# Attention slots in twos: unscaled exponentials are turned, and the reciprocals of the row sums go round by DRAM to the outputs' rows

## The reference

```python
xn = layernorm(x)
# attention
q = xn @ wq.T; lat = xn @ w_kv_down.T; k = lat @ w_k_up.T; v = lat @ w_v_up.T   # 16 heads of 64
q, k = rope(q), rope(k)
probs = softmax(q @ k.T / sqrt(64) + causal_mask)
s = concat_heads(probs @ v) @ wo.T
# experts
logits = xn @ gate_w + gate_b
e = max(top2_indices(logits))
y = gelu(xn @ w1[e] + b1[e]) @ w2[e] + b2[e]
out = x + s * silu(2 * y)
```

## Time and profile before

| | |
|---|---|
| median of 3 runs | 310.14 us (309.95 to 311.69) |
| the profiled execution's own time | 310.5 us |
| its span | 308.7 us |
| PE, busy share of the span | 95% |
| ACT, DVE, POOL | 79%, 72%, 70% |
| mean granted clock of PE | 0.998 |

### The profile page before, as it was taken

One profiled execution on the slowest core, in us unless ns is written; L12 is line 12 of the kernel. 1 busy time (PEld: TensorE's weight loads), 2 busy tenths in 40 slices (PEclk: granted clock), 3 DMA queues, 4 the chain that ended last, 5 costly groups with the idle time before them and its releaser, 6 DMA issues.

```text
span 308.7 us, 8487 instructions
## 1 busy us (share of the span) xinstructions
PE 294.3 (95%) x2362; PEld 235.4 (76%) x2362; DVE 221.0 (72%) x883; ACT 242.9 (79%) x851; POOL 215.9 (70%) x321
## 2 busy tenths in 40 slices
PE   8897999999999999999999989999989999899994
PEld 3566878888888888777777789999867777786763
DVE  3889998987787998988887523323278789898651
ACT  3387889898887889999897665555799999889982
POOL 3378878786786879999999933332138999889730
PEclk9999999999999999999999999999999999999999
DMA  6764595979333333333345470000063334344200
GB/s 204 232 140 112 107 308 124 225 168 302 74 69 71 68 71 89 92 87 87 99 104 134 129 197 0 2 2 0 3 187 71 93 102 115 103 108 133 71 19 17
DMA packets 39596, 33.35 MB, mean 108 GB/s; under 512 B 4801, under 2 KB 36674, under 8 KB 39554
## 3 DMA queue, kind: packets, MB, share of 16 engines
q1 hardware_dynamic: 38098, 30.51, 38.3%
q0 software_dynamic: 1024, 2.10, 2.5%
q10 hardware_dynamic: 432, 0.23, 0.3%
HBM read 11.07 MB, written 4.98 MB: 52 GB/s over the span
## 4 chain that ended last, share of the span: by engine, by line
PE 64%; POOL 12%; issue 11%; DVE 8%; ACT 2%; DMA 1%; POOLq 1%; SPq 0%; DVEq 0%; ACTq 0%
PE bank L1092 9%; PE bank L1080 8%; PE bank L1106 7%; PE bank L1120 6%; PE bank L1285 6%; PE bank L1300 6%; POOL probs L474 5%; POOL staged L463 4%; PE bank L1054 3%; DVE rot_out L585 3%; PE bank L1108 3%; PE bank L1082 3%; DVE masked L594 2%; PE bank L1188 2%; PE bank L1070 2%
## 5 line engine op out<-in xcount | busy, mean ns | idle before, releaser
L885 ACT ACTIVATE pexp<-masked,negmax 128x128 f32<-128x128 f32 (+1 forms) x256 | 114.1, 452 | 1.5 <-DVE negmax L594 1.4
L474 POOL TENSOR_SCALAR probs<-pexp,rden 128x256 f32<-128x256 f32 (+1 forms) x184 | 80.3, 451 | 26.0 <-DVE rden L601 23.3
L594 DVE CUSTOM_DVE_ANT_0 masked<-bank,mask 128x128 f32<-128x128 f32 (+1 forms) x256 | 75.9, 351 | 27.1 <-PE bank L1082 26.9
L463 POOL TENSOR_TENSOR staged<-rot_out 128x512 f32<-128x512 f32 x63 | 80.2, 1275 | 17.8 <-DVE rot_out L585 17.3
L585 DVE TENSOR_TENSOR rot_out<-bank,rot 128x1024 f32<-128x1024 f32 x64 | 77.6, 1214 | 4.0 <-PE bank L1056 2.7
L907 ACT COPY probsT<-bank 128x384 f32<-128x384 f32 x128 | 54.9, 480 | 22.9 <-PE bank L1092 21.9
L1092 PE MATMUL bank<-ident,probs 128*128 128x128 f32 x384 | 54.7, 275 | 1.8 <-ACT probsT L907 0.9
L885 ACT ACTIVATION_READ_ACCUMULATOR pexp<-masked,negmax 128x1 f32 x256 | 49.9, 195 | 0.0
L1080 PE MATMUL bank<-qk_sb 64*128 64x256 f32 x256 | 45.0, 427 | 2.9 <-DVE negmax L594 2.1
L1092 PEld LDWEIGHTS bank<-ident,probs 128*128 128x128 f32 x384 | 43.1, 140 | 5.2 <-POOL probs L474 1.9
L1120 PE MATMUL bank<-vo_sb,ctxT 128*128 128x128 f32 x256 | 39.4, 278 | 0.7 <-ACT ctxT L914 0.7
(11 more groups left out here) (113 smaller groups left out, 458.1 us busy)
## 6 DMA issues: line engine op xcount, KB each, us to landing
qk_sb<-staged SPq DMA_DIRECT2D x128, 128.0 KB, 2.5
w_sb<-in_w SPq DMA_DIRECT2D x2, 1024.0 KB, 5.6
w_sb<-in_w SPq DMA_DIRECT2D x4, 512.0 KB, 4.9
sorted_x<-z SPq DMA_DIRECT2D x1, 1408.0 KB, 7.9
sorted_g<-z SPq DMA_DIRECT2D x1, 1152.0 KB, 5.5
out<-res SPq DMA_DIRECT2D x8, 128.0 KB, 1.8
x_sb<-in_x SPq DMA_DIRECT2D x3, 256.0 KB, 3.8
rot<-in_c_rot SPq DMA_DIRECT2D x1, 512.0 KB, 5.0
```

The costliest lines, as they stand in the source:

```text
L463: pool.tensor_tensor(staged[:, n % 2, :, m % 2, :], rot_out[:, m % 2, :, 0:S], rot_out[:, m % 2, :, S:2 * S], op=ALU.add).then_inc(staged_ ...
L474: pool.tensor_scalar(probs[:, g % 2, i, c], pexp[:, g % 2, i, c], rden[:, g % 2, i, k:k + 1], 1.0, ALU.mult, ALU.mult).then_inc(probs_read ...
L594: t = dve.tensor_tensor_reduce(masked[:, g % 2, i, c], s_bank[i][:, c], mask[:, c], -1.0, -NEG * 1e8, ALU.add, ALU.min, negmax[:, g % 2, i ...
L885: e = act.activation(pexp[:, g % 2, i, c], masked[:, g % 2, i, c], ACT.Exp, bias=negmax[:, g % 2, i, k:k + 1], scale=-1.0, accum_out=rowsu ...
```

## The change

Slots from 24 on go in **couples** (`g` even, `g` and `g + 1`), one call of `couple(g)` on each engine in place of two of `slot`.

- PE: `scores_of_two(g + 2)` runs the four large matmuls of both slots and then the four corners, which now go to `t_bank`. Behind them stand the outputs of slots `g - 4` and `g - 3`, then a projection, `turn(g)`, the other projection, `turn(g + 1)`, and `values(g - 2)`.
- In slots 24 to 61 the exponentials are turned as they are (`pexp`), with no `scale`. DVE forms the contexts' copy and multiplies it by `shares`, the reciprocals laid along the rows (`ctx_out`, now one operation of 128x512 on DVE and none on ACT). Slots 62 and 63 are still scaled.
- `shares` comes by DRAM. SP writes the 128x8 reciprocals of a couple so that each number is an element of its own (`rows_out`), waits until they have landed, and reads them back spread over 64 partitions in two DMAs (`rows_back`).
- DVE takes the maxima in two steps, `corner_max` of both slots first and `rest_max` of each later. `turn(g)` waits for both corners to be read.
- `TWICE` is (23, 25), so two projections come earlier. Slots 38, 39, 62 and 63 are no longer alone.
- At the end of the couple of slot 38 `values(38)` uses a bank of the scores, and the second part of `load` has a semaphore of its own, `xs_rest`, and stands behind the `place` of the couple.

```diff
-TWICE = (36, 38)
+TWICE = (23, 25)
...
-ALONE = tuple(range(FIRST_DOUBLE)) + (G_LEAD - 2, G_LEAD - 1, B * NP - 2, B * NP - 1)
+ALONE = tuple(range(FIRST_DOUBLE))
+LAST = B * NP - 2
...
+def scaled(g):
+    return g < FIRST_DOUBLE or g >= LAST
...
+            def rows_out(u):
+                sp.wait_ge(rden_ready, 2 * u + 2)
+                sp.dma_start(share_rows[u].rearrange("n i k p -> p (n i k)"),
+                             rden[:, u % 2].rearrange("p n i k -> p (n i k)"),
+                             allow_slow_non_contiguous=True).then_inc(row_out, 16)
+            def rows_back(u):
+                sp.wait_ge(row_out, 16 * (u - UNIT + 1))
+                if u < UNIT + 2:
+                    sp.wait_ge(probsT_done, 2 * FIRST_DOUBLE)
+                else:
+                    sp.wait_ge(ctx_ready, values_through(2 * u - 4))
+                for i in range(2):
+                    sp.dma_start(shares[HD * i:HD * i + HD, u % 2],
+                                 share_rows[u, :, i].rearrange("n k p -> n (k p)").unsqueeze(0)
+                                 .broadcast_to([HD, 2, S])).then_inc(row_in[u % 2], 16)
...
+            def couple(g):
+                if g == G_LEAD - 2:
+                    sp.wait_ge(scattered, 16 * NT)
+                    load(0, 4, xs_in)
+                if g < LAST:
+                    rows_out(g // 2)
+                    rows_back(g // 2)
+                for m in (*items(g), *items(g + 1)):
+                    if m % 2:
+                        place(m // 2)
+                if g == G_LEAD - 2:
+                    load(4, NR, xs_rest)
+                for n in (g, g + 1):
+                    if n in FINALS:
+                        store(FINAL_ORDER.index(FINALS[n]))
...
+            def corner_max(g):
+                dve.wait_ge(scores_done, g + 1)
+                dve.wait_ge(exp_done, 2 * g - 6)
+                for i in range(2):
+                    t = dve.tensor_tensor_reduce(corner(g, i), t_bank[i][:, g % 2 * P:(g % 2 + 1) * P], mask[:, 0:P],
+                                                 -1.0, -NEG * 1e8, ALU.add, ALU.min, negmax[:, g % 4, i, 0:1])
+                t.then_inc(corner_read, 1)
+            def rest_max(g):
+                dve.wait_ge(exp_done, 2 * g - 2)
+                for i in range(2):
+                    dve.tensor_tensor_reduce(masked[:, g % 2, i, P:SW], s_bank[i][:, g % 2 * S:(g % 2 + 1) * S], mask[:, P:SW],
+                                             -1.0, -NEG * 1e8, ALU.add, ALU.min,
+                                             negmax[:, g % 4, i, 1:2]).then_inc(masked_ready, 1)
...
+            def ctx_out(g):
+                u = g // 2
+                dve.wait_ge(pv_done, values_through(g))
+                dve.wait_ge(y_step, g + 2 - NP)
+                o, heads = v_bank(g)[:, 0:2 * S], ctxT[:, g % NP:g % NP + 2, :].rearrange("p n s -> p (n s)")
+                if scaled(g):
+                    dve.tensor_copy(heads, o).then_inc(ctx_ready, 1)
+                else:
+                    dve.wait_ge(row_in[u % 2], 32 * ((u - UNIT) // 2 + 1))
+                    dve.tensor_tensor(heads, o, shares[:, u % 2].rearrange("p n s -> p (n s)"),
+                                      op=ALU.mult).then_inc(ctx_ready, 1)
+            def couple(g):
+                if g - 4 >= FIRST_DOUBLE and g not in (G_LEAD, G_LEAD + 2):
+                    ctx_out(g - 4)
+                if g < LAST:
+                    corner_max(g + 2)
+                    corner_max(g + 3)
+                denominators(g + 1)
+                if g == LAST:
+                    scale(g + 1)
+                if g < LAST:
+                    rest_max(g + 2)
+                for m in items(g):
+                    rotate(m)
+                if (g + 1) // NP < LEAD and (g + 1) % NP == 3:
+                    take_y((g + 1) // NP - 1)
+                if FINALS.get(g + 1, -1) >= LEAD:
+                    finalise(FINALS[g + 1])
+                if g < LAST:
+                    rest_max(g + 3)
+                    denominators(g + 2)
+                if g + 2 == LAST:
+                    scale(g + 2)
+                for n in range(g, g + 2):
+                    if FINALS.get(n, LEAD) < LEAD:
+                        finalise(FINALS[n])
+                if g in (G_LEAD - 2, LAST):
+                    ctx_out(g - 2)
+                for m in items(g + 1):
+                    rotate(m)
             def finish(b):
+                ctx_out(NP * b + NP - 2)
...
             def exponentials(g, i):
                 act.wait_ge(masked_ready, 2 * g + i + 1)
+                if g >= FIRST_DOUBLE + 2:
+                    act.wait_ge(probsT_done, 2 * g + i - 3)
+                    act.wait_ge(rden_ready, g - 1)
                 for k, c in enumerate(rows):
-                    wait(act, probs_ready[i][k], g - 1)
-                    e = act.activation(pexp[:, g % 2, i, c], masked[:, g % 2, i, c], ACT.Exp,
-                                       bias=negmax[:, g % 2, i, k:k + 1], scale=-1.0,
+                    if g < FIRST_DOUBLE + 2:
+                        wait(act, probs_ready[i][k], g - 1)
+                    e = act.activation(pexp[:, g % 2, i, c], masked[:, g % 2, i, c] if k else corner(g, i), ACT.Exp,
+                                       bias=negmax[:, g % 4, i, k:k + 1], scale=-1.0,
                                        accum_out=rowsum[:, g % 2, i, k:k + 1])
                 e.then_inc(exp_done, 1)
-
...
-                act.copy(ctxT[:, g % NP:g % NP + n, :].rearrange("p n s -> p (n s)"),
-                         o_bank[:, 0:n * S]).then_inc(ctx_ready, 1)
+                wait(act, y_step, g + 1 - NP)
...
+            def couple(g):
+                if g == FIRST_DOUBLE:
+                    exponentials(g + 1, 0)
                     ctx_out(g - 2)
-                if g == G_LEAD:
-                    exponentials(g + 1, 0)
-                ctx_out(g - 1)
-                if g == G_LEAD:
                     exponentials(g + 1, 1)
-                    scale(g + 1)
+                turned_probs(g)
+                if g < LAST:
+                    exponentials(g + 2, 0)
+                    if g != G_LEAD - 2:
+                        exponentials(g + 2, 1)
+                turned_probs(g + 1)
+                if g == G_LEAD - 2:
+                    exponentials(g + 2, 1)
+                if g < LAST:
+                    for i in range(2):
+                        exponentials(g + 3, i)
+                if g == FIRST_DOUBLE:
+                    ctx_out(g - 1)
...
+            def scores_of_two(g):
+                pe.wait_ge(masked_ready, 2 * g)
+                for n in range(2):
+                    p = (g + n) % NP
+                    pe.wait_ge(qk_in[p], 32 * (g // NP) + 32)
+                    for i, r in enumerate(half_rows):
+                        pe.matmul(s_bank[i][:, n * S:(n + 1) * S], qk_sb[r, 0, p, P:S], qk_sb[r, 1, p, :], start=True, stop=True)
+                pe.wait_ge(probsT_ready, 2 * (g - 2))
+                for n in range(2):
+                    p = (g + n) % NP
+                    for i, r in enumerate(half_rows):
+                        m = pe.matmul(t_bank[i][:, n * P:(n + 1) * P], qk_sb[r, 0, p, 0:P], qk_sb[r, 1, p, 0:P],
+                                      start=True, stop=True)
+                m.then_inc(scores_done, 2)
...
+            def couple(g):
+                ahead = (*items(g), *items(g + 1))
+                if g < LAST:
+                    scores_of_two(g + 2)
+                if g == FIRST_DOUBLE:
+                    output(g - 2)
+                elif g == FIRST_DOUBLE + 2:
+                    output(g - 3)
+                elif g not in (G_LEAD, G_LEAD + 2):
+                    output(g - 4)
+                    output(g - 3)
+                for m in ahead[:1]:
+                    project(m)
+                turn(g)
+                for m in ahead[1:2]:
+                    project(m)
+                if g == LAST:
+                    values(g - 2)
+                turn(g + 1)
+                for m in ahead[2:]:
+                    project(m)
+                if g == FIRST_DOUBLE:
+                    values(g - 1)
+                elif g not in (G_LEAD, LAST):
+                    values(g - 2)
+                if g == G_LEAD - 2:
+                    values(g)
...
             def finish(b):
                 g = NP * b + NP
+                output(g - 4)
+                output(g - 3)
                 if g == G_LEAD:
-                    output(g - 3)
-                output(g - 2)
-                values(g - 1)
-                if g == G_LEAD:
-                    pe.wait_ge(masked_ready, 2 * G_LEAD + 4)
                     pe.wait_ge(xs_in, 16)
                     turn_tile(0, 0)
+                else:
+                    values(g - 2)
+                output(g - 2)
                 output(g - 1)
```

173 lines of the change are left out of this document (85 added, 88 removed).

## The result

The changed kernel takes **464.22 us** (median of 4 runs, 463.76 to 464.79) beside 310.5 for the kernel before (four runs now): ratio 1.494 (95% interval 1.489 to 1.499). I had said 314, range 303 to 330. Medians and ranges are of all executions of a kernel, a ratio is of those within 1.5% of its fastest, and a time with no range beside it is of a single execution.

What follows compares the result with a forecast made beforehand. PE's own stream bounded the kernel before; the new couples were to follow a 6.88 us loop. Terms +3.5 - 0.5 + 2.0 - 1.3 = +3.7 on 310.5 gave 314.2, from the median 313.8, said as 314, range 303 to 330.

Steps and rivals of the forecast that it cites:

- D: Time from issue to landing of the store of a couple's reciprocals, which SP waits out: taken as 3.3 us.
- small elements dear: Rival: storing 4-byte pieces costs more than reading them; D 4.8, SP's round 8.7, total 333 to 337 us; chance 0.17.
- SP's round as D + 3.9: SP's queue per couple: the store's landing, then reads and place; 7.2 us against a couple of 6.9.
- the way to the experts: Slots 24 to 39: SP's rounds put the eighth `rows_out` at 171.4 and delay the experts by 3.5 us.
- The stream of 6.53: PE's own work per couple if nothing waits: fewer array changes take 0.40 us out of 6.93.
- The loop of 6.88: From `turn(g)` to `turn(g + 2)` over ACT, DVE and PE: 6.88 us a couple, outputs waiting 0.35.
- step 1: Loop's start on ACT: copy 0.58 after the transpositions, second at most 0.43 later, exponentials some 0.38 behind: 1.33 us.
- The experts' start at 180.1: Experts start behind `shares` at 178.25, `ctx_out(38)` at 178.95 and PE's last outputs (1.05), against 176.65 before: +3.5 us.
- D + 3.15: Time from the start of `rows_out` until the reciprocals read back have landed as `shares`.
- Behind the experts: Deferred outputs of three slots -0.5 us, six couples from 44 to 54 +2.0, couples 56, 58 and 60 -1.3.
- the end: The kernel's last stretch, one store behind one `finalise`, claimed to stay as before.
- waits on `shares` in every couple, and couples of 8 us or more: Sign in the profile after that would show the small elements rival, chance 0.17.

Runs made afterwards that it cites:

- two edits: On the 32 B version, rotate ahead of the last reciprocals: 320.67 us. The whole change with 16 B pieces and a strided multiplication: 327.41 us.
- the version with the fast store: The changed kernel with a couple's reciprocals stored as 128 pieces of 32 B instead of 1024 of 4 B, output wrongly scaled: 319.91 us.
- mended: Whole change with 16 B pieces (327.41 us), plus rotate, couple 38's store, ACT's copies of slots 40 and 41, and `ctx_out(58)` moved earlier: 321.21 us.
- finals: `mended` with DVE's finalise moved ahead of the couple's second rotate: 319.68 us.

## Why the prediction was wrong

1. **D, the landing of the reciprocals' store, is the step that failed.** I put it at 3.3 and closed the range at 3.8, by the load of 1024 small elements; it took 9.3 to 12.9, median 10.5. The bound was from a *read* of DRAM. The piece count was the same, but a load does not write 16 pieces into 64 B of DRAM; at one piece in 64 B the store did take 3.4. I named the rival (small elements dear), gave it 0.17 and held it at D of 4.8, less than half of what came; and the range ended at 330, below that rival's own 333 to 337.
2. **SP's round as D + 3.9** held in the changed kernel: 10.95 + 3.9 is 14.85, and 14.90 is in the rows. Put into my own working of the way to the experts, the eighth `rows_out` comes at 118.4 + 7 x 14.4 + 2.6 = 221.8 with the median (222.68 in the trace) and the experts start at 237.6 (0.4, 10.5, 3.15, 0.7 and 1.05 behind it); they start at 239.49, 62.8 later than before. From slot 40 to the end are 175.8 us against 85.8, 90 more. It did not hold beside quicker 4 B stores: with D at 3.4, near my own figure, the rounds were 8.1, the experts started at 188.33 and the kernel took 335.65, outside the range. So the right D alone would hardly have brought 314. The 22 us between were not taken apart further; that run also reads a table in place of the reciprocals.
3. **The stream of 6.53** was right in kind, 0.10 short (6.63). **The loop of 6.88** was right: 6.90 with a fast store, and it answered to two edits as a loop does. The wait there is 0.19 in the rows against my 0.35. (The parts of its step 1 are 0.58, at most 0.43, and 0.38, so up to 1.39; I wrote 1.33.)
4. **The experts' start at 180.1** is 180.22 in the version with the fast store, and that is luck. Its store of couple 38 starts at 170.27 and not 171.8; from there to `ctx_out(38)` are 7.34 us and not D + 3.15 = 6.45; and PE's outputs behind it, at half clock after a wait of 5.07, take 1.87 and not 1.05. With the store at 3.4 the start was 188.33.
5. **Behind the experts** I had -0.5, +2.0 and -1.3. With the fast store, slots 40 to 44 take 14.60 us against 13.08 before: the deferred outputs give nothing. PE's corners wait for ACT's copy of slot 41, which stands behind the `Silu`, a table load and the exponentials of 42 (PE's timeline of that version):

```profile
235.35 0.71 PE L1226 MATMUL bank<-qk_sb 64*128 64x128 f32 x8 [1.76 <-ACT probsT L1041]
```

   Most of the 1.5 us is PE's clock behind that wait, 0.74 in the mean from 235.35 to 241.87. In the run with pieces 64 B apart the same wait is 1.75 and the clock behind it 1.00, and the slots take 13.29. `mended`, with both copies ahead of the exponentials, takes 13.09 at a clock of 1.00: PE waits 1.96 there for DVE's maxima instead, so ACT's order is worth 0.2. `finals` has that wait at 1.94, a clock of 0.52 behind it, and 14.55.

   The couples 44 to 56 take 43.1 against 42.4 (+0.7). And the end, which I said "stays", takes from slot 60 20.5 us against 17.6: `ctx_out(58)` stands on DVE behind the scaling of 62, and PE waits 2.22 for it; with it earlier, in `mended`, the end takes 19.7. From slot 56 to 60 it is 13.05 against 12.69. With the entry (+3.6) and the experts themselves (+0.8, with PE's clock at 0.95 from 177 to 225 where it was 1.00) these are the 9.9 us by which the span of 318.6 stands above 308.7, where my sum had 3.7.
6. **That the store does nothing but hold SP**, which the working assumed without saying it, was wrong too: unwaited it costs 42 us.
7. **PE's clock has no term in the sum.** It was 0.998 before and is 0.838 in the changed kernel. With the fast store it is 0.984, and the outputs ahead of the experts, the experts and slots 40 to 44 paid for it.

What the profile would show: "waits on `shares` in every couple, and couples of 8 us or more" is what came, at 15.

## What to carry to other kernels

A round trip through DRAM on a DMA queue is priced by its landing, and the landing by the layout in DRAM, not by bytes or pieces alone: 4 KB took 2.3 us as 32 B pieces and 10.5 as 4 B neighbours. Bound a cost that the trace does not show from a row of the same direction, and where there is none leave the upper end open. When an engine that is 95% busy is relieved, follow the loop of all the engines behind it step by step: here it gave 6.9 us for a stream of 6.6, and what was won in the middle was lost at the seams, part of it to PE's clock behind a wait.

## What the runs showed of the hardware

- Writes of 4 B into the same 64 B of DRAM: 1, 4, 8 and 16 to a stretch took 3.4, 4.0, 6.1 and 10.5 us for 1024 pieces (issue of the store to SP's next issue, medians of 19 in one trace each).
- Issued on the same queue behind an unwaited store of 1024 neighbouring pieces of 4 B, a copy of 128 KB landed after 6.24 us, where 2.5 is the median without such stores.
- A DVE multiplication of 128x512 with one operand at a stride of 16 B in SBUF: 1080 ns against 681.
- DVE's addition with both operands in SBUF takes 1.75 us in place of 0.42 when POOL's addition runs at the same time, and the wait lies inside DVE's own record. The Trainium skill, "SBUF — State Buffer", SBUF: two separate sides, says that a DVE operation with two SBUF inputs and a GpSimd one that reads SBUF take turns on a port, each for its whole length, the one that starts first going first. The trace agrees that one waits the other out: DVE's record ends 0.28 to 0.29 behind POOL's. It does not bear out who goes first, by the records' starts: DVE was the one that waited where its record starts 0.28 behind POOL's (265.80) and also where it starts 0.17 ahead (275.55).
- Behind waits of 4.76, 5.07, 6.94 and 7.31 us PE's granted clock stood at 1.2 GHz: from 152 to 156, behind the wait of 6.94 that ends at 152.20, it is 0.50 in the mean, from 156 to 160 0.98. Behind waits of 1.94 and 1.76 it fell too (0.52 and 0.74 in the mean of the stretch), behind others of 1.96 and 1.75 in the same place of the kernel it stayed at 1.00.
